# Moving the late half of a first MoE across a program boundary, with one shared tile's products left ahead of it

## The reference, cut to what matters

```python
def ffn(h):      # twice, with the same weights
    probs = softmax(h @ router_w + router_bias); top 2 of 16, normalised -> combine
    routed = combine[:, 15:16] * h + sum_e combine[:, e:e+1] * ((silu(h @ gate_w[e]) * (h @ up_w[e])) @ down_w[e])
    shared = (silu(causal_conv3(h)) * (h @ shared_up_w)) @ shared_down_w
    return shared + routed
def attn(x):     # two layers of a retention block
    for i in range(2):
        q, k, v, xo = split(layer_norm(x) @ proj_w[i] + proj_b[i])
        ret = ((q @ k.T) * decay) @ v                  # 16 heads of 16
        x = x + (ret * silu(xo)) @ reto_w[i] + reto_b[i]
        x = x + gelu(layer_norm(x) @ ffn1_w[i] + b1) @ ffn2_w[i] + b2
    return layer_norm(x)
x = x + 0.5 * ffn(layernorm(x)); x = x + attn(layernorm(x)); x = x + 0.5 * ffn(layernorm(x))
```

## Time and profile before

| what | value |
|---|---|
| three runs | 1435.53, 1438.24, 2847.57 us; median 1438.24 |
| the profiled execution | 1436.97 us, its span 1435.2 us |
| mean granted PE clock | 0.976 |
| busy | PE 92%, DVE 70%, ACT 43%, POOL 40% |
| the Block of the first MoE ends, the retention begins | about 312 to 315 us from the span's start |
| SP's three tables issued; the first pair's matmuls begin | 5 to 9 us; 98 us |

### The profile page before, as it was taken

The page is one execution under the profiler, slowest core; times in us unless marked ns, Lnnn a source line. Parts: engine busy times, 40 slices in busy tenths (PEclk is TensorE's granted clock), DMA queues, the critical chain, the costliest instruction groups (busy, mean ns, idle before and its releaser), DMA issues.

```text
span 1435.2 us, 30723 instructions
## 1 busy us (share of the span) xinstructions
PE 1321.7 (92%) x11824; PEld 1087.4 (76%) x11824; DVE 1008.5 (70%) x2390; ACT 614.5 (43%) x1034; POOL 573.0 (40%) x460
## 2 busy tenths in 40 slices
PE   5959998856999999999999899999999999999998
PEld 2449988435888788788788688788788776699974
DVE  5756465377977877876876867877887868655745
ACT  4726555411343333333434344333333656666641
POOL 0536270631323332331441533552553436272635
PEclk9979999978999999999999999999999999999999
DMA  9977695920000000000001000000000038586845
GB/s 324 382 233 247 214 345 205 305 90 1 2 2 2 1 2 1 2 1 2 34 12 61 2 1 2 16 16 1 16 16 1 31 97 302 192 272 214 272 134 154
DMA packets 113628, 150.99 MB, mean 105 GB/s; under 512 B 12240, under 2 KB 96080, under 8 KB 113488
## 3 DMA queue, kind: packets, MB, share of 16 engines
q1 hardware_dynamic: 99088, 113.36, 24.0%
q0 software_dynamic: 12288, 33.57, 7.1%
q10 hardware_dynamic: 2112, 2.10, 0.4%
HBM read 77.56 MB, written 71.43 MB: 104 GB/s over the span
## 4 chain that ended last, share of the span: by engine, by line
PE 61%; DVE 14%; ACT 1%; issue 1%; POOL 0%; DVEq 0%; ACTq 0%
PE l_w_ps L84 9%; PE l_w_ps L86 8%; PE l_w_ps L85 8%; DVE l_probs L2060 5%; PE l_banks L2322 4%; PE l_rm_ps L2354 3%; PE l_banks L84 2%; PE l_banks L85 2%; PE l_banks L86 2%; PE l_rm_ps L2347 2%; PE b_gu_ps L84 2%; PE b_gu_ps L85 1%; PE b_gu_ps L86 1%; DVE l_f_lo L2091 1%; PE b_t_ps L1312 1%; DVE l_full L2022 1%
## 5 line engine op out<-in xcount | busy, mean ns | idle before, releaser
L2060 DVE TENSOR_TENSOR l_probs<-l_banks,l_past 128x512 f32<-128x512 f32 x256 | 160.0, 682 | 35.4 <-PE l_banks L2322 35.3
L1820 ACT ACTIVATE l_act_f<-l_w_ps,l_ffn_b 128x512 f32<-128x512 f32 x120 | 82.6, 689 | 170.5 <-PE l_w_ps L86 165.7
L84 PE MATMUL l_w_ps<-l_w_hi,l_f_hi 128*128 128x256 f32 x496 | 143.7, 290 | 2.6 <-DVE l_f_lo L2091 2.4
L1911 POOL TENSOR_TENSOR l_g_lo<-l_q,l_g_hi 128x1024 fp32r<-128x1024 f32 x16 | 38.2, 2387 | 267.0 <-ACT l_g_hi L1811 267.0
L85 PE MATMUL l_w_ps<-l_w_lo,l_f_hi 128*128 128x256 f32 x496 | 139.6, 282 | 0.0
L86 PE MATMUL l_w_ps<-l_w_hi,l_f_lo 128*128 128x256 f32 x496 | 139.5, 281 | 0.0
L84 PE MATMUL l_w_ps<-l_b_hi,l_w_hi 128*128 128x512 f32 x240 | 102.5, 427 | 0.3 <-ACT l_f_hi L1821 0.3
L1898 POOL TENSOR_TENSOR l_q_wide<-l_q,l_pair_mask 128x1024 f32<-128x1024 f32 x32 | 60.1, 1896 | 103.5 <-DVE l_q L2038 103.5
L812 POOL DMA_INDIRECT rows<-a_xn,a_pos_i x64 | 65.9, 1030 | 86.4 <-DVE a_pos_i L975 67.5
L84 PEld LDWEIGHTS l_w_ps<-l_w_hi,l_f_hi 128*128 128x128 f32 x496 | 93.3, 188 | 8.8 <-issue 8.7
L2091 DVE TENSOR_TENSOR l_f_lo<-l_act_f,l_f_hi 128x512 fp32r<-128x512 f32 x128 | 85.7, 702 | 18.3 <-ACT l_f_hi L1821 18.3
(11 more groups left out here) (428 smaller groups left out, 4000.1 us busy)
## 6 DMA issues: line engine op xcount, KB each, us to landing
rows<-a_zeros SPq DMA_DIRECT2D x14, 1024.0 KB, 12.9
a_xb<-rows SPq DMA_DIRECT2D x46, 256.0 KB, 3.4
rows<-a_yb SPq DMA_DIRECT2D x46, 256.0 KB
b_xb<-rows SPq DMA_DIRECT2D x46, 256.0 KB, 3.3
rows<-b_yb SPq DMA_DIRECT2D x46, 256.0 KB, 3.1
a_w_in<-in_moe_w SPq DMA_DIRECT2D x15, 384.0 KB, 9.1
low_dram<-a_w_lo SPq DMA_DIRECT2D x15, 384.0 KB, 6.7
b_w_lo<-low_dram SPq DMA_DIRECT2D x15, 384.0 KB, 9.0
```

The source lines that it names most:

```text
L84: tensor.matmul(out, w_hi, x_hi, start=start, stop=False)
L1820: nc.scalar.activation(act_f[:, f, :], hidden_ps(b, f), ACT.Gelu, bias=ffn1_b[:, b.layer, f:f + 1]).then_inc(act_done, 1)
L2060: dve.tensor_tensor(probs[c % 2][:, r * w:(r + 1) * w].rearrange("p (h n) -> p h n", n=P), banks[:, r, :].rearrange("p (h n) -> p h n", n= ...
```

## The change

The late part of the first MoE, from tile 5's gate products on, is taken out of the first Block and put into the retention's Block, as generators that the retention's engine programs advance by `next(opening)`. The first Block now ends for PE behind tile 4's gate and up products, for ACT behind the evacuation of tile 5's transposes, for POOL behind column 15's pick, for DVE behind column 15's `combine` and two small copies (`wk_late`, `pos_late`), for SP behind the last result store and a wait for three early stores of x. The work ahead of tile 0's projection is now done by the retention's own functions. The semaphores of the moved part are those of the second MoE, which counts on from them (`turned_past`, `gated_past`, `shared_past`, `added_past`).

In detail:

- Front: SP loads tiles 0 and 2, then the three tables, then tiles 4 and 6; PE does turn 2 ahead of route 0, and turn 3 ahead of route 2.
- Loop: SP stores tiles 0, 1 and 2 of x inside the loop, at q = 35, 39 and 43 (`STORED_EARLY` = 3), instead of behind it.
- Second Block: SP loads two weight pieces, the 26 constants, five pieces, then stores the other tiles. DVE normalises tile 0 twice, then product 4, columns 16 and 17, one `low_home`, product 5, then waits for all constants, and scales tile 0 into `full`. PE turns tile 0 into the banks of tile 4's gate and up products, so tile 6's gate products wait for that scale (`first_full`). Tile 7's down products stand between the second and the third block of tile 0's projection.
- Columns 26 to 31 and the last two `low_home` are done inside step 0 of the retention, behind `gate_result` of c = 0, 1, 2; POOL picks the columns 30 and 31 between `widen_queries` and the memset of `v_wide`.
- In layer 0 PE now waits for the low weights as it did in layer 1 only.

```diff
@@ sync (first Block)
-                for t in range(0, NT, 2):
-                    sp.dma_start(x_sb[:, t * SUB:(t + 1) * SUB, :], tile_view(x_in, t)).then_inc(x_in_done[t], 16)
+                for t in range(0, 4, 2):
+                    load_tile(sp, t)
...
+            if begins:
+                for t in range(4, NT, 2):
+                    load_tile(sp, t)
...
+                for t in range(STORED_EARLY):
+                    if begins and q == COMBINE_FROM + (t + 1) * SUB + LAG:
+                        store(t)
...
+            if begins:
+                sp.wait_ge(stored_first, 16 * STORED_EARLY)
+                sp.wait_ge(low_kept, 16 * PIECES)
+                for of in range(HALVES):
+                    sp.wait_ge(cleared[of], 16 * sum(chunk[0] == of for chunk in chunks))
+                return
@@ tensor (first Block)
-                for t in range(4):
-                    turn(t)
-                    if t:
-                        route(t - 1)
+                turn(0)
+                turn(1)
+                turn(2)
+                route(0)
+                route(1)
+                turn(3)
+                route(2)
                 route(3)
...
             shared_in(FRONT)
+            if begins:
+                return
+        def tail_sync(sp):
+            for n, (w, _, _, src) in enumerate(pieces):
+                sp.dma_start(w, src).then_inc(home_in[n], 16)
+                if n == 1:
+                    for dst, const in consts:
+                        sp.dma_start(dst, const).then_inc(consts_in, 16)
+            for t in range(STORED_EARLY, NT - 1):
...
+        def tail_scalar(act):
+            yield
+            gate(4)
+            high_home(range(0, 2))
+            gate(5)
+            evacuate(6)
+            yield
+            high_home(range(2, 5))
+            gate(6)
+            evacuate(7)
+            high_home(range(5, len(pieces)))
+            gate(7)
+        def tail_vector(dve):
+            product(4)
+            combine(range(16, 18))
+            low_home(range(0, 1))
+            product(5)
+            dve.wait_ge(consts_in, 16 * len(consts))
+            yield
+            combine(range(18, 20))
+            yield
+            add(4)
+            low_home(range(1, 3))
+            combine(range(20, 21))
+            product(6)
+            combine(range(21, 23))
+            add(5)
+            combine(range(23, 24))
+            low_home(range(3, 4))
+            combine(range(24, 26))
+            product(7)
+            add(6)
+            low_home(range(4, 5))
+            add(7)
+            yield
+            combine(range(26, 28))
+            low_home(range(5, 6))
+            yield
+            combine(range(28, 30))
+            low_home(range(6, 7))
+            yield
+            combine(range(30, 32))
+        def tail_tensor(pe):
+            into(5)
+            pe.wait_ge(late.sh_done, 1)
+            yield
+            turn(6)
+            down(4)
+            freed(pe, "first_full")
+            into(6)
+            turn(7)
+            down(5)
+            into(7)
+            down(6)
+            pe.wait_ge(late.sh_done, NT - LATE_FROM)
+            yield
+            down(7)
+            yield
+            pe.wait_ge(late.shared_added, NT - LATE_FROM)
@@ retention, vector
+                opening = first_moe.vector(dve)
+                measure("0", whole(0))
+                normalise_0(whole(0))
+                measure("1", whole(0))
+                normalise_1(whole(0))
+                next(opening)
+                scale(aT_done, banks[:, KD:2 * KD, :], norm1, a_full, whole(0))
+                next(opening)
+                low_first()
+                next(opening)
                 measure("0", whole(1))
@@ retention, tensor
+                opening = first_moe.tensor(pe)
+                next(opening)
+                pe.wait_ge(xn_done, 1)
+                turn(banks[:, KD:2 * KD, :], xn).then_inc(aT_done, 1)
+                next(opening)
                 project(whole(0), None)
@@ project
                     for m in range(2 * KD):
+                        if is_number(a, 0) and m == KD:
+                            next(opening)
                         project_block(a, banks[:, m, :], m)
+                    if is_number(a, 0):
+                        run(opening)
@@ retention, gpsimd
                 next(moe)
+                opening = first_moe.gpsimd(pool)
+                next(opening)
                 widen_queries(whole(0))
+                run(opening)
+                pool.memset(v_wide[:, :, :, :, :], 0.0).then_inc(wide_zero, 1)
```

More of the change, by code:

```diff
@@ L1208, in vector @@
-            low_home(range(2, 4))
-            finish(range(22, 24))
-            shared_product(7)
-            low_home(range(4, 6))
-            dve.wait_ge(first_turned, 1)
-            dve.wait_ge(consts_in, 16 * len(consts))
-            for k in range(KD):
-                last = dve.tensor_scalar(home.full[:, k, :], first_ps[:, k, :], home.norm1[:, 0, 0, k:k + 1],
-                                         home.norm1[:, 0, 1, k:k + 1], ALU.mult, ALU.add)
-            last.then_inc(first_full, 1)
@@ L1227, in tensor @@
+            shared_product(3)
+            finish(range(16, 19))
+            for t in range(4, NT - 1):
+                shared_product(t)
+                finish(range(4 * t + 3, 4 * t + 4))
+                add_shared(t - 1)
+                finish(range(4 * t + 4, 4 * t + (7 if t < NT - 2 else 6)))
+            shared_product(NT - 1)
+            add_shared(NT - 2)
+            finish(range(COLS - 2, COLS))
+            add_shared(NT - 1)
         def tensor(pe):
@@ L1328, in shared_down @@
                 else:
-                    pe.wait_ge(shared_added, t)
+                    pe.wait_ge(shared_added, shared_past + t)
                 if begins and t == 1:
-                    pe.wait_ge(xT_done, NT)
-                for s in range(SUB):
-                    last = pe.matmul(shared_ps[:, s, :], hidden(t)[:, s * P:(s + 1) * P], w_sh[:, down_at:down_at + D],
-                                     start=True, stop=True)
-                last.then_inc(s_acc_done, 1)
+                    pe.wait_ge(xT_done, turned_past + NT)
+                down_products(pe, t).then_inc(s_acc_done, 1)
             def turn_x(n):
```

412 lines of the change are left out of this document (219 added, 193 removed).

## The result

Seven runs of each kernel on one chip: the changed kernel's median is 1427.75 us (1425.07 to 1431.51), the kernel before's 1436.63. The ratio is 0.9946, 95% interval [0.9928, 0.9963], so the gain is 7.8 us by the ratio (8.9 between the medians), 0.5%: clear of zero, and well inside the 2% that would count as faster. One of the seven runs of the kernel before took 2847.57 us, and the ratio leaves this slow one out. The forecast was 1428. The profiled execution took 1425.07 us, span 1423.2, against 1436.97 and 1435.2: 12.0 less.

What follows compares the result with a forecast made beforehand. Late part taken as bound by DVE and cross-engine waits, the loop by DMAs. Masks 12.1 us earlier (with -0.4 front, +2.8 loop), +2.5 step 0: -9.6 on 1436.97 gives 1427.4, median 1428.7, forecast 1428; range 1419 to 1441.

Steps and rivals of the forecast that it cites:

- Front: Start of the kernel up to the logits: turn 2 fills PE's gap of 1.29 us before route 0, taken as -0.4 us.
- Loop: Experts' loop: early stores of x cost DMA time, two at 1.4 us each, +2.8; range 0 to 15.9.
- rival 3: Experts' loop: each early store sets off a stall, 5.3 us each, 15.9 in all, giving 1441, slower than before; chance 0.08.
- Boundary: Between first and second Block, behind PE's 257.7: the change of Block costs 2.5 us (2.1 to 3.4).
- Constants: Start of second Block: weights 1.2, issue of 26 constants 13.4, landing 3.0, so all are in 17.6 us after its start.
- B: The second Block's start, predicted at 257.7 + 2.5 = 260.2 us; later times there are counted from it.
- Rival 1: Second Block: constants come late, DVE's wait lasts to 23.6, PE's chain +6.0 us, giving 1434; chance 0.18.
- The chain behind the wait: Second Block, from tile 0's scale through tile 6's products (9.3 us) and the projection to the masks' end at B + 55.2.
- Step 0: Retention's first step: six columns and two splits come onto DVE, partly fitting into its waits; +2.5 us (0 to 7.9).
- Rival 4: Retention's first step: the move is only a move, the full 7.9 us is paid, +5.4, giving 1433; chance 0.07.

Runs made afterwards that it cites:

- group 1: Four kernels on a chip of their own beside the kernel before (1433.36 us): the changed kernel again (1428.28) and three edits of it, among them the old front (1429.69).
- the early stores alone: The kernel before, with only tiles 0 to 2 of x stored inside the loop: 1435.26 us, ratio 1.0006 to the kernel before.
- both boundary edits: Changed kernel with norm constants on their own semaphore and tile 4's gate and up products behind the boundary: 1416.01 us, ratio 0.9867; 1588.50, 0.9892 on the slower chip.
- the clearing first: On both boundary edits, GpSimd clears `v_wide` ahead of widening tile 0's queries: 1583.71 us, ratio 0.9851 on the slower chip.
- the splits later: On the clearing first, two splits of FFN2's weights moved behind c = 3 of step 0 and c = 0 of step 1: 1580.60 us, ratio 0.9848.

## Why the prediction was right, and where it was not

The median, the direction and the place are right: PE's wait of 11.3 us ahead of the projection went, and a shorter one for the constants came. That 1428 was met so closely is luck in part. In the first pair of profiles the gain up to the masks was 5.9 us larger than worked out (front 1.5, loop 3.9, boundary 1.1, and 0.7 lost in the chain behind it), and step 0 gave 3.6 more back. The largest of these, the loop's, is no wider than the scatter of that stretch between profiles. Term by term:

- **Front, -0.4.** The wait was right: turn 2 waits 0.90 for ScalarE's normalisation, 0.4 less than the gap of 1.29. Left out were the lengths of the matmuls behind it, 1.5 us shorter in the first pair: -1.9 in the first profile, -1.5 in group 1.
- **Loop, +2.8 (0 to 15.9).** The profiles stand at the lower end (151.8 us in the mean of nine for 152.1), the times of the early stores alone (1.0006) exclude rival 3 but not 2.8. The doubtful step is "the result stores come later by that": it makes DMA time into PE's time. With the stores alone PE is busy for 3.35 of the 5 us from 210 on, where it was 4.23, but 4.81 of those from 220 on, where it was 2.83; over the 25 us from 205 to 230 it is 21.16 against 21.23. The stall was already in the kernel before; counting it again per store gave rival 3. The Trainium skill (DMA: Bandwidth & Descriptors, "Issuing engines are not separate DMA queues") is not contradicted by this: the stall did move to the first store. Whether it has a price here the times don't tell.
- **Boundary, 2.5.** 1.39 on PE, below the range of 2.1 to 3.4; with tile 4's products behind it 2.53, of which 1.1 are ScalarE's evacuation. The lower rows that bounded it ran from VectorE's last work to GpSimd's first, and GpSimd begins later than PE (256.71 for 256.04); the 3.4 held PE's hand-made increments, which are gone.
- **Constants, 17.6 behind B.** 19.2 came out. Issue was right (0.9 and 13.6 for 1.2 and 13.4); landing was 4.7 for the 3.0 taken, inside the 1.8 and 6.8 that bounded it. Rival 1 (23.6) did not come. By the Trainium skill (DMA: Bandwidth & Descriptors, "Anatomy of one DMA"), an estimate of 2.3 us for 128 KB from a fit that the page gives for DMAs issued on GpSimd, the end would have been at 16.9. These loads are SyncE's, and the measurement, with 26 small DMAs, picks and weights in flight, is longer and decides.
- **The chain behind the wait.** Tile 6's products 8.6 for 9.3, since the clock was not at half for all of them (0.77 granted over the twelve). End of the masks from B: 52.8 + 2.4 = 55.2 predicted, 55.9 measured. That PE hangs on the constants is shown from two sides, -5.9 and -6.0 by the times, and together -17 against the kernel before.
- **Step 0, +2.5 (0 to 7.9).** It was +6.1 to step 1's first masks: the term that was mis-sized. Three parts. VectorE's idle time in that stretch was 5.75 us and took in 4.1, where the prediction counted on 7.9 - 2.5 = 5.4, though the three idle places that it named hold only 4.0 (1.49, 1.7 and 0.8). Behind that, more than half of each us is paid: 3.0 us less work give 1.7 to 3.1, two splits later give 2.5 for 2.3. The clearing of `v_wide`, costed at nothing because it is ready when `values` needs it, runs beside VectorE's normalisation and adds 1.7 to it. And 1.5 come behind, with a lower clock of PE; why the clock is lower there was not tried. Rival 4 (the full 7.9, 1433) was nearer for this stage than the forecast, but its mechanism, VectorE as the bound, was given 0.07.

As to what would show it: the wait for constants before `l_full` (6.88, some 5 predicted), PE's 8.28 in 6 to 9, and the projection without the 11 us and at full clock (1.00 granted from 296.44 to 302) came. The gap behind tile 4's products came at 1.39, not 2 to 3. Tile 6's products ran slowly, 7.01 for twelve, not the 7.75 of half clock. The masks ended at 312.0, not near 318, and the time from masks to `l_fresh` grew by 4.6, not 2.5.

The versions that beat both kernels: both boundary edits, 1416.01 where the kernel before has 1432.96; and on the slower chip the same with the clearing first and the splits later, 1580.60 for 1605.49, which takes ratio 0.9892 to 0.9848.

## What to carry to other kernels

When a wait for many small loads ends on the last of them, give those that the next instruction reads a semaphore of their own: here four of 26, worth 6 us by the times (3 in the profiled pair), as much as moving 7 us of other work into the wait, and both together more. A gap that an engine has for another is a store of time that is spent once; add up what the change puts into it and charge what goes over it. An instruction that nobody waits for is free only if its neighbour engine doesn't slow down beside it: put it where that neighbour is idle. And when an edit that should test one place also moves work at another, as the early stores did, read the time of both places before the total is believed.

## What the runs showed of the hardware that was not expected

- Beside GpSimd's own work on memory VectorE's `tensor_scalar` from SBUF to SBUF lasts longer. Beside the clearing of 128x1536 f32 (1.39 us), VectorE's four `tensor_scalar` of 128x256 f32 from SBUF to SBUF took 3.10 instead of 1.38. VectorE lost 1.7, more than the clearing itself lasts. Indirect DMA issues on GpSimd at the same time cost nothing (1.38 with picks beside it). Not all of VectorE's operations suffer: in the changed kernel its statistics from 315.31 on run beside GpSimd's addition of the bias (2.34 us from 315.27) and take the 0.42 and 1.06 that they take in the kernel before with GpSimd idle. A slowed `tensor_scalar` stands in the kernel before too, and the prediction did not use it; ahead of step 1's first masks, VectorE and GpSimd:

```profile
369.74 2.65 DVE L2002 TENSOR_SCALAR l_xn<-x_sb,l_mv,l_rstd 128x256 f32<-128x256 f32 x4
```

```profile
367.52 3.75 POOL L1898 TENSOR_TENSOR l_q_wide<-l_q,l_pair_mask 128x1024 f32<-128x1024 f32 x2 [5.29 <-DVE l_q L2038]
```

- PE's clock in this stage: behind 1.31 and 1.39 us idle twelve products took 5.42 and 5.39 (1.00 granted, 2.4 GHz, from the start), behind 4.91 they took 8.42 (0.64 granted), behind 8.28 and 8.10 idle 7.01 and 8.39 (0.77 and 0.64), and behind 2.53 in four profiles 7.05 to 7.09, in two others 5.39 (the kernels with the clearing first and with the splits later). So the length of the last idle time alone does not settle it.
- The end of one Block and the start of the next cost PE 1.4 us behind the last engine's last work. PE's idle time there is 1.39 in the six profiles in which tile 4's products stood ahead of the boundary and PE was that last engine, and 2.53 in the six in which it had only tile 5's turn there and ScalarE's evacuation of it ended 1.1 later (252.44, with PE on again at 253.81, where tile 4's products alone were moved).
- Issuing a 512 KB load took SyncE 0.41 us at the start of the second Block (0.82 for two), 0.84 (1.67 for two) behind one store of x and 1.68 (3.36 for two) behind four.
